# Three PSUM banks for the second scores and one for the preparations, in both attentions

## The reference

```python
# layer 0, second half (causal, 512 keys)
q, k, v = split(layernorm(x, ln1_g, ln1_b) @ Wqkv); q, k = (rope(q), rope(k))
scores = jnp.where(causal, jnp.einsum('bqhd,bkhd->bhqk', q, k) / math.sqrt(hd), -1e9)
attn = jnp.einsum('bhqk,bkhd->bqhd', softmax(scores), v).reshape(B, T, D) @ Wproj
# layer 1, first half (masked, 1024 keys of the context)
q, k, v = x @ Wq.T, ctx @ Wk.T, ctx @ Wv.T
scores = jnp.where(mask == 0, min_val, jnp.einsum('bhqd,bhkd->bhqk', q, k) * inv_scale)
ctx = jnp.einsum('bhqk,bhkd->bhqd', softmax(scores), v) ; return ctx @ Wo.T
```

## Time and profile before

| | us |
|---|---|
| median of 3 runs | 2823.77 (2822.34 to 2824.34) |
| profiled execution | 2824.32 |
| its span | 2822.5 |
| self attention, first preparation to the last second scores | 880 to 1227 |
| cross attention, the same | 1740 to 2442 |
| busy in the whole span | PE 1618.4, DVE 1707.8, ACT 922.7, POOL 262.0 |

### The profile page before, as it was taken

One profiled execution on the slowest core, in us unless ns is written; L12 is line 12 of the kernel. 1 busy time (PEld: TensorE's weight loads), 2 busy tenths in 40 slices (PEclk: granted clock), 3 DMA queues, 4 the chain that ended last, 5 costly groups with the idle time before them and its releaser, 6 DMA issues. The chain is left out here.

```text
span 2822.5 us, 33492 instructions
## 1 busy us (share of the span) xinstructions
PE 1618.4 (57%) x9827; PEld 923.9 (33%) x9906; DVE 1707.8 (61%) x7069; ACT 922.7 (33%) x1580; POOL 262.0 (9%) x225
## 2 busy tenths in 40 slices
PE   5940000000164888862596923899999999803675
PEld 2210000000163555532273713444444444402443
DVE  5329999999866878742010124766767677276554
ACT  1322211200001656530111101466666666412332
POOL 0000000000000000003100040000000000053432
PEclk8975555555586898985798966899999999956888
DMA  2130000010001000002405023010100000000000
GB/s 91 60 146 23 27 27 27 27 62 0 1 19 39 9 9 9 1 1 104 163 16 171 15 74 128 1 53 1 53 1 1 24 1 1 1 31 0 0 0 30
DMA packets 57114, 102.25 MB, mean 36 GB/s; under 512 B 7166, under 2 KB 40242, under 8 KB 55690
## 3 DMA queue, kind: packets, MB, share of 16 engines
q1 hardware_dynamic: 40272, 79.36, 8.0%
q10 hardware_dynamic: 13632, 13.63, 1.5%
q0 software_dynamic: 3072, 7.53, 0.8%
HBM read 68.54 MB, written 32.83 MB: 36 GB/s over the span
## 5 line engine op out<-in xcount | busy, mean ns | idle before, releaser
L948 DVE CUSTOM_DVE_ANT_0 xam_junk<-xam_s,xa_mask_q 128x512 bf16<-128x512 f32 x512 | 339.9, 687 | 177.6 <-PE xam_s L855 177.0
L1021 ACT ACTIVATE xam_exp<-xam_s 128x512 f32<-128x512 f32 x512 | 302.9, 598 | 213.4 <-PE xam_s L889 173.3
L565 PE MATMUL ps_e<-ident,span 32*128 32x32 f32 x2 | 0.4, 300 | 595.4 <-DMA span<-path_spans 595.4
L855 PE MATMUL xam_s<-xa_kT,xa_qT 96*128 96x512 bf16 x512 | 198.3, 390 | 15.4 <-DVE xam_max L948 9.6
L886 PE MATMUL xam_s<-xa_qT,xa_kT 99*128 99x512 bf16 x512 | 196.8, 384 | 7.7 <-ACT xam_exp L1021 7.0
L565 PEld LDWEIGHTS ps_e<-ident,span 32*128 32x128 f32 x2 | 0.3, 201 | 596.3 <-DMA span<-path_spans 596.3
L889 PE MATMUL xam_s<-xa_mask_k,identb 128*128 128x512 bf16 x433 | 165.0, 381 | 0.0
L379 DVE TENSOR_TENSOR_SCAN cost<-m,cost,dist_chunk 128x33 f32<-128x33 f32 x576 | 161.9, 281 | 0.0
L948 DVE CUSTOM_DVE_ANT_0 l0m_junk<-l0m_s,l_tri_q 128x128 bf16<-128x128 f32 (+3 forms) x256 | 121.2, 489 | 53.8 <-PE l0m_s L855 50.7
L416 ACT COPY near<-chunk_near 128x528 f16 (+1 forms) x37 | 39.8, 1075 | 306.0 <-DVE chunk_near L344 306.0
L900 PE MATMUL xam_o<-xam_exp,xa_vt 128*32 128x512 f32 x1024 | 137.2, 605 | 0.0
(11 more groups left out here) (315 smaller groups left out, 3833.4 us busy)
## 6 DMA issues: line engine op xcount, KB each, us to landing
dist<-stage SPq DMA_DIRECT2D x1, 9504.0 KB, 24.0
dist_chunk<-dist SPq DMA_DIRECT2D x36, 264.0 KB
ex_w<-L_ffn_W ACTq DMA_DIRECT2D x8, 1024.0 KB, 14.7
ex_w<-L_ffn_W SPq DMA_DIRECT2D x8, 1024.0 KB, 16.1
xa_mask<-mask_BxSxS_ik SPq DMA_DIRECT2D x4, 2048.0 KB, 10.4
ctx_nat<-ctx ACTq DMA_DIRECT2D x4, 1024.0 KB, 14.3
ctxT_d<-ctxT SPq DMA_DIRECT2D x4, 1024.0 KB, 8.2
ctx_rows<-ctx SPq DMA_DIRECT2D x1, 4096.0 KB, 14.1
```

Of the source, the lines that this page charges most:

```text
L855: nc.tensor.matmul(ps1[n % 2][:, 0:w], qT[0:STK, slot(g, h), qt * P:(qt + 1) * P], kT[0:STK, slot(g, h), f * 512:f * 512 + w], start=True, ...
L948: nc.vector.tensor_tensor_reduce(junk[:, n % NJ, 0:w], ps1[n % 2][:, 0:w], heads.bias_q(g, qt, f), 1.0, NEG * 4, ALU.add, ALU.max, mx[:, g ...
L1021: nc.scalar.activation(ebuf[at % NE][:, q0:512], ps2[at % 2][:, q0:512], ACT.Exp).then_inc(exped, 1)
```

## The change

Of the eight banks, one goes from the preparations to the second scores. `second` now waits for the exponentials of three units before instead of two. A round of preparation now waits until the readers of the round just before it are through. Nothing else is changed: the units, the order of work on each engine and the number of instructions that compute are the same.

```diff
-        self.bank = [nm.ps(f"prep{i}", [P, 512]) for i in range(2)]
+        self.bank = [nm.ps("prep", [P, 512])]
...
-            if rn >= 2:
-                for who in self.takers(self.rounds[rn - 2][2]):
-                    pe.wait_ge(self.freed[who], self.taken(who, rn - 2))
-            bank = self.bank[rn % 2]
+            if rn >= 1:
+                for who in self.takers(self.rounds[rn - 1][2]):
+                    pe.wait_ge(self.freed[who], self.taken(who, rn - 1))
+            bank = self.bank[0]
...
-        ps2 = [nm.ps(f"s2_{i}", [P, 512]) for i in range(2)]
+        ps2 = [nm.ps(f"s2_{i}", [P, 512]) for i in range(3)]
...
-                    if n >= 2:
-                        pe.wait_ge(exped, n - 1)
+                    if n >= 3:
+                        pe.wait_ge(exped, n - 2)
-                    o = ps2[n % 2]
+                    o = ps2[n % 3]
...
-                        nc.scalar.activation(ebuf[at % NE][:, q0:512], ps2[at % 2][:, q0:512],
+                        nc.scalar.activation(ebuf[at % NE][:, q0:512], ps2[at % 3][:, q0:512],
```

## The result

The changed kernel takes 2917.2 us (median of 4 runs, 2907.4 to 2920.7) against 2824.1 before: 93 us more, a ratio of 1.032, 95% interval 1.029 to 1.035. That is slower, as forecast, and inside the range, but 32 us above the forecast of 2885.

The account below looks back on a forecast made before the run. No engine full in the self attention, a loop of waits; TensorE nearly full in the cross attention. Self attention 33.6, cross 16.1, steps ahead 11.1: +60.8 on 2824.3, so 2885; range 2850 to 2925.

Parts of the forecast that it names:

- the clock case: Rival: more idle TensorE brings a second slow stretch into self attention steps, 2902; cross attention too, 2919; chance 0.14.
- the fourth wait: Self attention, second projection (unit 10): wait 1.17 hidden behind VectorE's work, costed at nothing; remainder 0.18 left to the range.
- the short waits: Self attention: two further preparation rounds wait briefly, left to the range without a stated size.
- absorbed: Rival: VectorE or ScalarE catches up, half the self attention's waits and of 13.6 count; 2861 or 2850, chance 0.20.
- the three waits: Self attention steps: both turns of k and first projection wait 0.96, 1.10, 0.34; 2.40 a step, +33.6 over 14.
- The stretches ahead: Two steps ahead of each attention: self attention +4.8, cross attention's first pass +6.3, its second nothing; together +11.1.
- The cross attention's steps: Waits at second turns of q, k and the mask's turn, +13.6, +4.0, +6.2, less 7.7 from the third bank: +16.1.
- the wait of 0.55: Cross attention, unit 25: TensorE's wait for an exponential, removed by the third bank; 14 x 0.55 = -7.7.
- The one place where the change does what it is for: Cross attention, unit 25: only there does the third second-score bank save time, 7.7 us over 14 steps.

Follow-up runs that it names:

- the run with one and two: Against the changed kernel: one preparation bank kept, but two instead of three banks of second scores, in both attentions; 2925.9 us, ratio 1.037.
- the run with the last turn apart: One preparation bank, two second-score banks; in the self attention the second turn of k alone gets the unused bank, against that kernel without this; 2888.7 us.

## Why the prediction came out as it did

The direction and the size are right, but that 2917 lies in the range is partly luck. It is outside what the forecast itself took (2865 to 2905) and above the clock case (2902). The upper end, 2925, was called that case with the fourth wait's remainder and the short waits; the remainder is 14 x 0.18 = 2.5 us, and for the other 20 no wait was named. The largest miss, 24 us ahead of the attentions, stood in none of the rivals.

- **The direction and the mechanism: right.** Each new wait stands where the timeline of before put it, in both attentions. The third bank is worth 9 us against 102 for the preparation bank (shown by the run with one and two). The case "absorbed" is out: the maximum at L948 is 3.4 late, not less than the three waits (2.40). That the fourth wait is hidden is shown twice, by the timeline and by the run that removed it.
- **The self attention's steps, 2.40 each: a little short.** At full clock a step grew by 22.25 - 19.34 = 2.91, 40.8 in 14 steps. The 0.5 that lacks are the second turn of q (0.2, which I had left to the range) and, by the timeline, some 0.1 at each wait between the end of the copy and the start of the matmul, which I had taken as zero by adding start and duration. The 0.16 in the run with the last turn apart is probably the same.
- **The clock in these steps: the rival, in another form.** I had it as a second slow stretch at 1.2 us. It was the existing one that grew, from 3.4 us (7.0 in two of the 14 steps) to 6.8. A step with one cost 1.1 more before and costs 1.6 more now; over the steps the clock's share is 48.5 - 40.8 = about 8 of the 15 us missed here, in this execution; in that of the change in the self attention alone, 323.4 - 282.1 = 41.3, it is under 1. It did not come to the cross attention's steps, which keep 1.00 but for the first (12.4 us at the lower level, 9.4 before). The rule of the Trainium skill that stood beside the rival (TensorE: Matmul & The Clock Gate, A second HAM failure mode: psum-queue depth-cycling), that short idling at each turn of the banks makes the clock swing, holds here in the self attention and ahead of both, and not in the cross steps, whose TensorE is busy 41.4 of 44.3 us. In the kernel before, though, it was the waits for the turned maxima that brought the slow stretch, and no turn of a bank.
- **The stretches ahead, 11 instead of 35: the term that failed.** Two steps of its reasoning did. I priced them at the waits of a steady step, but there is no other work of TensorE between the rounds, so every round waits out its copy: in the first pass of the cross attention the matmuls' waits sum to 11.8 us against 4.5 before, and the pass is 13.7 longer. And I took nothing for the second pass since VectorE's maxima set its pace; it took 7.4 more, with VectorE as busy as before (27 of 41 us now) and TensorE 5.8 us busier at a lower clock. That a stretch with a granted clock of 0.77 has more to lose was in the trace; I had read the clock in the steps only. The run with two banks ahead shows that all 35 hang on the bank there; how they split between waiting and clock is read from busy times and is an estimate.
- **The cross attention's steps: close.** +19.1 against 16.1. The missing preparation bank cost 23.9 (the kernel with one and two), where the terms had 23.8; the third bank gave 4.8 instead of 7.7. That term counted the wait of 0.55 in 14 steps, where the earlier trace rows have it 8 times and 4.4 us in all: a slip in reading the rows. In the plain steps the bank gave 0.8, in those with mask turns, which have no such wait, 0.1.
- **The last two steps of each attention: not counted.** They have no preparations, so only the gain is left: 2.2 and 3.2.
- **"The one place where the change does what it is for":** right, the third bank takes that wait away. But it was not needed for it: with the rounds spaced two banks have no such wait either. I had not asked what else would remove it.

## What to carry to other kernels

Where a bank goes from two to one, price each round by the timeline (start of its matmuls against the end of the last reader) and then do it again for the stretches without other work for that engine, which have the least cover and the lowest clock; a steady step says nothing of them. Before a buffer is given more banks, ask what the engine that it waits for does first; if that can be moved, it costs no bank. And read the granted clock of each stretch along with its length: ahead of the steps here TensorE's new idle time cost, by estimate, about as much again in slowed matmuls.

## What of the hardware was not expected

- Useless work made the kernel faster: 30 matmuls of 128 columns a step in TensorE's idle places held the granted clock at 1.00 and took 1.2 us off each step of 20.5 (2811.0 against 2822.7 us).
- Filling one of two idle places didn't keep the clock: the stretch at the 1.2 GHz level moved from the start of the step to behind the next idle place and halved, from 6.8 to 3.4 us, with the step at 23.9 us as before.
- The slow stretch has no fixed length here: 3.4 us of most steps in the kernel before and 7.0 of two, 6.8 in the changed one, and with the same code 98.4 us of 14 steps in one execution and 67.5 in another. What sets which of the two it is, and why some steps have none with the same order of work (22.3 us at 958 beside 23.9 at 1004), was not settled.
